# Two-point interpolation of gathered rows: row and difference in the table, one weighting pass, three turned pieces a chunk instead of six

## The reference, cut to what matters

```python
pos = jnp.clip(pos, 0.0, Ll - 1.0)
lo = jnp.floor(pos).astype(jnp.int32)
hi = jnp.minimum(lo + 1, Ll - 1)
frac = pos - lo.astype(x.dtype)
g_lo = xh[b_ix, lo]
g_hi = xh[b_ix, hi]
g = g_lo + frac[..., None, None] * (g_hi - g_lo)
out_h = jnp.einsum('blshd,blhs->blhd', g, w)
```

## Time and profile before

| | us |
|---|---|
| median of 3 runs (2652.23 to 2656.2) | 2653.66 |
| profiled execution, device time | 2654.81 |
| its span, first to last instruction | 2653.0 |
| TensorE busy, share of the span | 1890.1, 71% |
| VectorE busy | 1313.9, 50% |
| ScalarE busy | 968.4, 37% |
| GpSimd busy | 1122.5, 42% |
| mean granted TensorE clock, share of 2.4 GHz | 0.816 |

### The profile page before, as it was taken

The page is one execution under the profiler, slowest core; times in us unless marked ns, Lnnn a source line. Parts: engine busy times, 40 slices in busy tenths (PEclk is TensorE's granted clock), DMA queues, the critical chain, the costliest instruction groups (busy, mean ns, idle before and its releaser), DMA issues.

```text
span 2653.0 us, 35007 instructions
## 1 busy us (share of the span) xinstructions
PE 1890.1 (71%) x12481; PEld 1295.4 (49%) x12481; DVE 1313.9 (50%) x2253; ACT 968.4 (37%) x2371; POOL 1122.5 (42%) x1131
## 2 busy tenths in 40 slices
PE   3867677596766875977767758777677547787795
PEld 1834344285543542854435527544355225565564
DVE  4265453255656743556566535475575343333325
ACT  2045355302453443024535540145355322222342
POOL 0000000266644752656347516564475057777400
PEclk9588798767898897668988986689799868878986
DMA  3000000222322332223223323222233233333202
GB/s 103 1 12 17 8 17 13 51 80 81 94 66 72 95 78 57 78 81 94 66 68 96 85 48 85 82 86 70 62 106 86 72 72 103 100 102 98 76 0 56
DMA packets 95398, 180.17 MB, mean 68 GB/s; under 512 B 21352, under 2 KB 52208, under 8 KB 94960
## 3 DMA queue, kind: packets, MB, share of 16 engines
q0 software_dynamic: 50688, 138.48, 18.7%
q1 hardware_dynamic: 44528, 39.34, 5.1%
HBM read 152.57 MB, written 8.39 MB: 61 GB/s over the span
## 4 chain that ended last, share of the span: by engine, by line
PE 39%; DVE 28%; ACT 11%; issue 10%; POOL 9%; DMA 2%; SPq 1%; DVEq 0%; POOLq 0%; ACTq 0%
POOL pool_c L646 9%; DVE pool_c L1096 4%; PE c L1431 4%; PE sc L1289 4%; PE ta L1348 3%; PE pb L1369 3%; PE pa L1327 3%; DVE ssq L1001 3%; DVE pool_a L1063 3%; DVE pool_a L1066 3%; PE pb L1327 2%; ACT prob L773 2%; DVE nmax L1011 2%; DVE pool_a L1054 2%; ACT pool_a L749 1%
## 5 line engine op out<-in xcount | busy, mean ns | idle before, releaser
L646 POOL DMA_INDIRECT pool_c<-rows_of_x,idx x1056 | 1063.7, 1007 | 1365.5 <-DVE idx L1164 724.5
L1096 DVE TENSOR_TENSOR pool_c<-pool_c 128x768 f32<-128x768 f32 x352 | 336.6, 966 | 321.7 <-DMA pool_c<-rows_of_x,idx 254.3
L1431 PE MATMUL c<-ident,pool_c 128*128 128x128 f32 x2112 | 349.2, 314 | 62.3 <-DVE pool_c L1096 62.2
L1431 PEld LDWEIGHTS c<-ident,pool_c 128*128 128x128 f32 x2112 | 293.3, 165 | 161.4 <-issue 89.7
L695 ACT COPY pool_a<-ta 128x512 f32<-128x512 f32 x200 | 119.1, 595 | 282.3 <-PE ta L1348 147.0
L773 ACT ACTIVATE prob<-sc,nmax 128x128 f32<-128x128 f32 x512 | 180.3, 379 | 26.5 <-DVE nmax L1011 25.7
L1001 DVE TENSOR_REDUCE ssq<-pool_a 128x16 f32<-128x1024 f32 x64 | 78.0, 1219 | 207.1 <-ACT pool_a L749 207.1
L1348 PE MATMUL ta<-ident,rinv 128*64 128x128 f32 x1024 | 84.6, 317 | 108.2 <-DVE rinv L1016 90.6
L1327 PE MATMUL pa<-wqkv,pool_a 128*128 128x512 f32 x216 | 139.2, 732 | 11.1 <-DVE pool_a L891 11.1
L848 ACT ACTIVATE prob<-prob 128x512 f32<-128x512 f32 x64 | 40.3, 630 | 252.9 <-DVE prob L1134 252.9
L1327 PE MATMUL pb<-wqkv,pool_a 128*128 128x512 f32 x168 | 106.1, 718 | 33.2 <-DVE pool_a L1054 22.6
(11 more groups left out here) (344 smaller groups left out, 3612.0 us busy)
## 6 DMA issues: line engine op xcount, KB each, us to landing
pool_c<-rows_of_x,idx POOLq DMA_INDIRECT x1056
vmix<-vring SPq DMA_DIRECT2D x128, 128.0 KB, 2.4
rows_of_x<-x2tok SPq DMA_DIRECT2D x8, 512.0 KB
xtok<-in_x SPq DMA_DIRECT2D x4, 512.0 KB, 3.9
x_of_all<-x2tok SPq DMA_DIRECT2D x4, 512.0 KB, 3.3
x2tok<-x_of_all SPq DMA_DIRECT2D x8, 256.0 KB, 3.0
out<-pool_a SPq DMA_DIRECT2D x8, 256.0 KB, 2.4
wqkv<-in_wqkv SPq DMA_DIRECT2D x1, 1536.0 KB
```

The lines of the kernel that those rows point to most:

```text
L646: pool.indirect_dma_start(gat[:, n % GB, s, :], None, table, bass.IndirectOffsetOnAxis(ap=idx[:, t, SC * c + s:SC * c + s + 1], axis=0),). ...
L1096: V.tensor_tensor(g4, g4, wv, ALU.mult).then_inc(SEM["c_prod"], 1)
L1431: ins = mm(out[:, c:c + P], x, ident[:], start=(i == 0 and k == 0), stop=(i == BCH - 1 and k == len(parts) - 1), is_transpose=True, skip_g ...
```

## The change

The table holds x2[r] and x2[r+1]-x2[r] (zero for the last token). The difference is made by VectorE in column layout (step `dx`), turned by TensorE in two more blocks and copied by ScalarE (steps `dxt`), and written by its own 512 KB DMA; the two small DMAs are gone. `dx` and its turned form lie in `gat`. A new list order puts `dx` first and `dxt` behind `x2t`; the head has 14 steps in place of 12.

For a chunk VectorE now runs three `scalar_tensor_tensor` instructions of 128 columns, row + f x difference, into one of three buffers `mix`, waits for them, and multiplies the 384 columns by the head weights, read straight from `wk`. TensorE turns three pieces. GpSimd's step `w` and `wlh` are gone. A buffer of `gat` is free when VectorE has interpolated it (`c_mix`), and VectorE waits ahead of chunk n until TensorE has added chunk n-3. `positions` has 12 instructions in place of 13.

```diff
+GB = 5
+MB = 3
-    steps = [("x2t", j) for j in range(J)] + [("wk", t) for t in range(T)] + [("pos",), ("w", 0)]
+    steps = [("dx",)] + [("x2t", j) for j in range(J)] + [("dxt", j) for j in range(J)] + [("wk", t) for t in range(T)] + [("pos",)]
-            if n % NCH == NCH // 2 and n // NCH + 1 < T:
-                steps.append(("w", n // NCH + 1))
-HEAD = 2 + T + 2
+HEAD = 1 + 2 * J + T + 1
...
# SP
-                    sp.dma_start(table[1:N + 1, 0:D]..., x2tok[:])
-                    sp.dma_start(rows[0:N]..., x2tok[:])
-                    sp.dma_start(table[0:1, 0:D], x2tok[0:1, 0, :])
-                    sp.dma_start(rows[N:N + 1], x2tok[P - 1:P, T - 1, :])
+                    half, src = (0, x2tok) if what == "x2t" else (1, dxtok)
+                    sp.dma_start(table[:, D * half:D * (half + 1)]..., src[:])
# GpSimd
-                    chunk_added(pool, b, n - GB)
+                    wait(pool, "c_mix", b, SC * (n - GB + 1))
-                elif what == "w":
-                    ...
# VectorE
+                if what == "dx":
+                    wait(dve, "ln_out", b, 8)
+                    V.tensor_tensor(dx[:, 0:N - 1], x2[:, 1:N], x2[:, 0:N - 1], ALU.subtract)
+                    V.memset(dx[:, N - 1:N], 0.0)
-                    if c == 0:
-                        wait(dve, "c_w", b, t + 1)
-                    g4 = gat[:, n % GB].rearrange("p s (c h d) -> p (s c) h d", c=2, h=H)
-                    wv = ap3(wlh[:, t % 2, SC * c, 0, :], [[H, 2 * SC], [1, H], [0, HD]])
-                    V.tensor_tensor(g4, g4, wv, ALU.mult).then_inc(SEM["c_prod"], 1)
+                    if n >= MB:
+                        chunk_added(dve, b, n - MB)
+                    for s in range(SC):
+                        g = gat[:, n % GB, s, :]
+                        V.scalar_tensor_tensor(mix[:, n % MB, s, :], g[:, D:2 * D], frac[:, t, SC * c + s:SC * c + s + 1], g[:, 0:D],
+                                               ALU.mult, ALU.add).then_inc(SEM["c_mix"], 1)
+                    wait(dve, "c_mix", b, SC * (n + 1))
+                    m4 = mix[:, n % MB].rearrange("p s (h d) -> p s h d", h=H)
+                    wv = ap3(wk[:, t, 2 * H + SC * c:], [[1, SC], [S, H], [0, HD]])
+                    V.tensor_tensor(m4, m4, wv, ALU.mult).then_inc(SEM["c_prod"], 1)
# TensorE
+                elif what == "dxt":
+                    wait(pe, "c_dx", b, 2)
+                    out = wait_free(pe, ("dxt", j), b)
+                    turn_tiles(out, lambda i: dx[:, BLK * j + P * i:BLK * j + P * (i + 1)])
-                    parts = [gat[:, n % GB, s, D * h:D * (h + 1)] for s in range(SC) for h in range(2)]
+                    parts = [mix[:, n % MB, s, :] for s in range(SC)]
```

More of the change, by code:

```diff
@@ L227 @@
 SECOND_KEYS = {
-    "pos": lambda: [], "w": lambda t: [], "g": lambda n: [], "cT": lambda j: [],
+    "pos": lambda: [], "dx": lambda: [], "g": lambda n: [], "cT": lambda j: [],
     "acc": lambda n: [(("sum", n // BCH), ("c0",))] if n % BCH == 0 else [],
     "co": lambda j: [(("co", j), ("c1",))],
-    **{k: (lambda k: lambda i: [((k, i), CB)])(k) for k in ("x2t", "wk")},
+    **{k: (lambda k: lambda i: [((k, i), CB)])(k) for k in ("x2t", "dxt", "wk")},
 }
@@ L392, in build @@
         tmp = pos
-        frac = part("c", T * S, 2)
+        frac = part("c", T, S)
         idx = sb("idx", [P, T, S], U32)
-        wlh = part("c", 2, S, 2, H)
         gat = part("c", GB, SC, 2 * D)
+        mix = part("c", MB, SC, D)
+        turned = gat.rearrange("p n s d -> p (n s d)")
+        dx, dxtok = turned[:, 0:N], turned[:, N:2 * N].rearrange("p (t d) -> p t d", d=D)
         zc = part("c", TB, D)
@@ L430, in build @@
         tri = pool_a[:, 8 * N:8 * N + P]
-        table = nc.dram_tensor("rows_of_x2", (N + 1, 2 * D), F32, kind="Internal").ap()
+        table = nc.dram_tensor("rows_of_x2", (N, 2 * D), F32, kind="Internal").ap()
         x3_dram = nc.dram_tensor("x3_of_all", (B * N, D), F32, kind="Internal").ap()
@@ L565, in second @@
             def second(b, what, *a):
[L566 to L576, removed]
+                if what in ("x2t", "dxt") and a[0] == J - 1:
+                    wait_drained(sp, (what, J - 1), b)
+                    wait(sp, "c_mix", b, 0)
+                    half, src = (0, x2tok) if what == "x2t" else (1, dxtok)
+                    sp.dma_start(table[:, D * half:D * (half + 1)].rearrange("(t p) d -> p t d", p=P), src[:]).then_inc(SEM["c_table"], 16)
                 elif what == "co" and a[0] == J - 1:
@@ L652, in second @@
                 if what == "pos":
-                    wait(pool, "c_pos", b, 13)
-                    wait(pool, "c_table", b, 64)
+                    wait(pool, "c_pos", b, 12)
+                    wait(pool, "c_table", b, 32)
                     for n in range(GB - 1):
                         gather(b, n)
-                elif what == "w":
[L659 to L666, removed]
                 elif what == "g":
@@ L800, in second @@
                     copy_out(("x2t", j), x2tok[:, TB * j:TB * (j + 1), :], b, tiles(TB))
+                elif what == "dxt":
+                    j, = a
+                    copy_out(("dxt", j), dxtok[:, TB * j:TB * (j + 1), :], b, tiles(TB))
                 elif what == "pos":
@@ L1080, in second @@
             def second(b, what, *a):
-                if what == "wk":
+                if what == "dx":
+                    wait(dve, "ln_out", b, 8)
+                    V.tensor_tensor(dx[:, 0:N - 1], x2[:, 1:N], x2[:, 0:N - 1], ALU.subtract).then_inc(SEM["c_dx"], 1)
+                    V.memset(dx[:, N - 1:N], 0.0).then_inc(SEM["c_dx"], 1)
+                elif what == "wk":
                     t, = a
@@ L1111, in second @@
                     if j == 0:
-                        wait(dve, "c_table", b, 64)
+                        wait(dve, "c_table", b, 32)
                     for t in range(TB * j, TB * (j + 1)):
@@ L1415, in second @@
                     turn_tiles(out, lambda i: x2[:, BLK * j + P * i:BLK * j + P * (i + 1)]).then_inc(full(("x2t", j)), 1)
+                elif what == "dxt":
+                    j, = a
+                    wait(pe, "c_dx", b, 2)
+                    out = wait_free(pe, ("dxt", j), b)
+                    turn_tiles(out, lambda i: dx[:, BLK * j + P * i:BLK * j + P * (i + 1)]).then_inc(full(("dxt", j)), 1)
                 elif what == "wk":
```

11 lines of the change are left out of this document (5 added, 6 removed).

## The result

The changed kernel takes 2738.19 us (median of 4 runs, 2736.2 to 2741.69); the kernel before took 2654.58 beside it. The ratio is 1.0317 with a 95% interval of 1.0299 to 1.0335: slower by 84 us, where 7 us faster were forecast and the range ended at 2685. The profiled execution took 2736.2 us, its span 2734.3.

The account below looks back on a forecast made before the run. No engine was full, so the chain of waits was taken as the bound, with 42 weighting chunks a turn on it. Three turns at +3.0 us and the tail's -16 gave -7: 2647 us, range 2612 to 2685.

Parts of the forecast that it names:

- VectorE per chunk: In the loop, a chunk costs VectorE 1.37 us in place of 0.87, 0.50 more (ends 0.35 and 0.66).
- How many chunks pay it: In a turn, 42 chunks on the chain pay, +21.0 us; the 46 off it add only +2 for lacking slack.
- Rival 2: VectorE becomes the bound through the attention stages, 21 more chunks paying: turn +16.7, time 2688; chance 0.19.
- TensorE per chunk and the clock: TensorE turns three pieces, not six: -15.9 us a turn; its clock falls from 0.82 to 0.80: +5.
- rival 3: TensorE's clock falls to 0.78: 10.7 us a turn, time 2664; sign, 0.50 from 1095 to 1143; chance 0.12.
- upper end: Clock loss of +13 a turn if L1348 and the projections behind it run at low level in eight more tiles.
- First chunk and head: At a turn's start, VectorE's first chunk waits for 3 gathers, not 12 and `w`: -9.1 us, head delay +1.8 included.
- Buffers: GpSimd's earlier release of `gat` is worth nothing, and VectorE's new wait for the addition of chunk n-3 costs nothing.
- rival 4: The wait for chunk n-3 ties VectorE to TensorE: some +10 us a turn, time 2677; chance 0.06.
- The tail: After the turns, `w` and waits go, -22; VectorE's longer work beside gathers +3.5, head 3: -16 us.

Follow-up runs that it names:

- e13: The changed kernel with GpSimd again waiting for TensorE's addition before gathering into a `gat` buffer, on a fast chip: 2735.2 us, 1.0317 of the kernel before.
- e14: The changed kernel with GpSimd waiting for TensorE's addition and without the head-weight multiply, fast chip: 2602.7 us, 0.9807 of the kernel before.
- e15: The changed kernel with GpSimd waiting for TensorE's addition and each piece turned twice, fast chip: 2739.9 us, 1.0315 of the kernel before.
- e10: The changed kernel with four buffers of `mix` in place of three, on a slow chip: 1.062 of the kernel before.

## Why the prediction was wrong, by its own steps

**VectorE per chunk: the price was right.** 1.37 forecast, 1.38 measured; the three instructions take 0.87 together where 0.86 was the sum. The rule of the Trainium skill ("VectorE: DVE Perf Modes", "The DRAIN you can't avoid"), weighed there, would have given 1.53: the three of 0.346 in 0.87 speak against it for operations with no wait between them.

**How many chunks pay it: one of the two steps that failed.** "On the chain lie 36.2/0.87 = 42 chunks a turn" was read rightly: the chain of before passes through 43. What failed is the sentence behind it, "A chunk off the chain (46) falls into an idle VectorE and costs nothing until its slack is gone", with +2 for the slack that some lack. Removing the multiply is worth 58 to 65 chunks in full (e13, e14), and in the changed kernel some 56 lie on the chain: some 13 had less slack than 0.5 us and joined it. For 0.51 more a chunk, 58 to 65 chunks are 30 to 33 us a turn, where 23 were forecast with the slack. Rival 2 named this mechanism, and its sign: a turn of over 548 us was its mark, and 563 came. It too was too small, 17 us a turn against 28.

**TensorE per chunk and the clock: the other step that failed.** -15.9 and +5, so -10.9 a turn, were forecast; e13 and e15 show -1.6, with 4 us of uncertainty, for the pieces and what the clock gives back for them. The 1056 pieces that are left are busy for 222 us, where 175 were forecast. In the chain of the turn the additions did go from 31.7 to 13 us, as forecast, but TensorE's other work there grew by 12 us. The clock's fall was sized at 0.82 to 0.80; it was 0.82 to 0.77 over the run, below even rival 3's 0.78, and it fell in every slice. In the heads stage, where 21 us of additions were thought to be worth half of that, the changed kernel came out of the stage with 1.5 us less lead than it had going in. The stretch with L1287, busy (PE, PEld), clock, DMA share, GB/s, answering to the earlier trace rows:

```profile
1117.00:1165.00 48.00, 24.79 (x112) 24.73 (x112) 0.50 0.34 101
```

That is 0.221 us a matmul, exactly the 28.32/128 of the stage without any additions, where with six pieces it had been 0.183. So rival 3's mark came, 0.50: half of the way back was taken where in this stage all of it came. The Trainium skill ("TensorE: Matmul & The Clock Gate", "What's actually happening") has the low rate as the default, which activity lifts. Within one stage the trace agrees: with the additions halved the heads went from 0.65 to 0.58, with all six back to 0.62 (e15), and the run's mean from 0.772 to 0.800. Across stages TensorE's busy share doesn't order the clocks: the heads are busy 91% (73.35 of 81 us) at 0.58, the last slice 69% at 0.83.

Part of the clock's fall comes from VectorE and not from the pieces. In an attention tile TensorE's step behind `rinv` takes 1.09 us at the high level (2.4 GHz) and 1.97 at the low one (1.2 GHz). It took over 1.2 in 5 of the 16 tiles before, in 10 after and in 9 with all six pieces back (e15), but in only 6 without the multiply (e14). The ninth tile, before and then after; the granted clock was 1.00 over the first two lines and 0.50 over the last two:

```profile
1389.63 1.09 PE L1348 MATMUL ta<-ident,rinv 128*64 128x128 f32 x16 [1.80 <-DVE rinv L1016]
1390.65 1.13 PE L1327 MATMUL pb<-wqkv,pool_a 128*128 128x512 f32 x2
...
1424.48 1.97 PE L1346 MATMUL ta<-ident,rinv 128*64 128x128 f32 x16 [3.49 <-DVE rinv L1006]
1426.38 2.08 PE L1325 MATMUL pb<-wqkv,pool_a 128*128 128x512 f32 x2
```

The prediction had this only as its upper end, "in eight more of the 16 tiles"; five more came.

**First chunk and head: right, or nearly.** -9.1 forecast. VectorE's first chunk of the second turn:

```profile
1078.70 0.93 DVE L1090 SCALAR_TENSOR_TENSOR pool_c<-pool_c 128x128 f32<-128x128 f32 x3 [7.03 <-DMA pool_c<-rows_of_x,idx]
```

7.0 us idle in place of 16.8, TensorE 5.4 in place of 14.0, and the turn is 8 us ahead at this point.

**Buffers.** That the new wait ties VectorE to TensorE (rival 4) is refuted: 26 us in the run, and a fourth buffer gained nothing (e10). That GpSimd's earlier release is worth nothing held on the fast chip (e13). On the slow chip it costs 126 us, by a mechanism of which the trace of before, taken on a fast chip, has no sign.

**The tail.** -16 forecast, -2 measured. GpSimd's waits did go (2.1 us are left), but the gathers got slower: from first to last 348 us, where "within 338" was the mark. Busy time of the 264 gathers, in the changed kernel and then in e14 (us, count, clock, DMA share, GB/s):

```profile
2220.00:2570.00 350.00, 268.88 (x264) 0.73 0.36 99
...
2098.00:2438.00 340.00, 251.39 (x264) 0.75 0.36 102
```

They took 257.0 before. The term was +3.5 for VectorE's longer work; it is +12, and it vanishes with the multiply: 17.5 us of gathers beside 88 multiplies. The Trainium skill ("GPSIMD Engine Reference", "Specifications") says that GpSimd shares its SBUF interfaces with VectorE and contends with instructions that have two SBUF inputs. The multiply is one; so are the three L1090, with which e14's gathers are yet faster than before, so the rule alone doesn't size it.

**The sum again, with what was measured.** Head -24, VectorE 3 x 30 to 33 = +90 to +99, pieces and clock -5, tail -2: +59 to +68, against +84 measured. Some 16 to 25 us, 5 to 8 a turn, are assigned to nothing. Tiles at the low level are a candidate: from `rinv` to the next L1001 or L991 ten tiles of the second turn take 54.6 us, 49.4 before. No run separates this from the rest, and the uncertainty of e13's and e15's medians (some 12 us) covers part of it too. Of the 91 us between forecast and result, the count of chunks is 21 to 30, the pieces with the clock 28, the tail 14 and the first chunk 3.

## What to carry to other kernels

The chain of waits says where time went, not how many instances of an instruction matter when it grows: those on the chain are the least number. Count also the instances inside the stages in which its engine takes part in a ring of hand-overs, and measure how much slack each has against the time that is added. In a chain with short pieces of a line followed by "issue", the line's share is too low. Before work is taken from a TensorE that runs below full clock, look at the clock with and without that work in the same stage, and expect that little of the saving may be left while the clock can fall further. An interpolation that halves the work of one engine by four small instructions on another pays only if the second engine isn't the one that closes the ring; here the same change without its multiply was 49 us faster than before.

## What the runs showed of the hardware

- Chips differ by 6% for the kernel before and by 9% for the changed one, and not in the speed of the instructions compared: the weighting of before is 1.82 for two and a gather 0.95 on both kinds. What differs is idle time without a releaser, 8 to 11 us against 144 to 259 on TensorE.
- On such a chip an edit can cost what it doesn't cost elsewhere: the early release of `gat` cost 126 us on one and nothing on the other (1.0317 with and without).
- 1056 matmuls of 128 columns added to 11457 cost 5 us of time and 79 us of busy time, with the mean clock rising from 0.772 to 0.800.
- Gathers issued by GpSimd took 0.95 us each on average without the multiply beside them (251.39/264) and 1.02 with it.
